# Expert layers in tiles of 128 slots, with each expert's split weights kept in a ring and rows scattered into slot order

## The reference, cut

```python
# L0: 16 experts, 4 choices, inner size 256, and one shared expert
scores = sigmoid(xf @ gate_w.T); s = scores + gate_bias
...
comb = zeros((T, E)).at[arange(T)[:, None], idx].add(weights)
h = silu(einsum('td,eid->tei', xf, w1)) * einsum('td,eid->tei', xf, w3)
y = einsum('tei,edi,te->td', h, w2, comb)
z = silu(xf @ ws1.T) * (xf @ ws3.T) @ ws2.T        # the shared expert
# L1: 8 experts, 2 choices, inner size 1024
topk_scores, topk_idx = top_k(einsum('btd,ed->bte', x, gate_w), 2)
hidden = silu(h1) * h2                # h1, h2: halves of x @ w12[e].T
y = sum(softmax-weighted hidden @ w3[e].T)
x = x + y + z                         # xf, x above: layer norm of x
```

## Time and profile before

| | us |
|---|---|
| median of 3 runs | 2283.02 |
| lowest, highest | 2277.21, 2283.86 |
| the profiled execution, own time | 2267.15 |
| its span in the trace | 2264.7 |

### The profile page before, as it was taken

One profiled execution on the slowest core, in us unless ns is written; L12 is line 12 of the kernel. 1 busy time (PEld: TensorE's weight loads), 2 busy tenths in 40 slices (PEclk: granted clock), 3 DMA queues, 4 the chain that ended last, 5 costly groups with the idle time before them and its releaser, 6 DMA issues. The chain is left out here.

```text
span 2264.7 us, 44300 instructions
## 1 busy us (share of the span) xinstructions
PE 1938.3 (86%) x16818; PEld 1669.7 (74%) x16818; DVE 1024.7 (45%) x1792; ACT 950.6 (42%) x1594; POOL 911.7 (40%) x655
## 2 busy tenths in 40 slices
PE   6876898738999991999999999777849999999993
PEld 5445676537999991788888888555639999999993
DVE  5445443465555566133333333355534445454442
ACT  2112333415666662233333333343425555555551
POOL 0004321006777774433333333221016666566653
PEclk9897999868999996999999999867869999999997
DMA  6562010007888885211011010100035566565653
GB/s 246 215 242 79 20 57 1 21 21 281 277 281 276 281 264 201 67 39 39 28 37 37 28 37 19 43 6 24 1 115 208 203 215 214 201 218 203 214 187 120
DMA packets 102161, 298.19 MB, mean 132 GB/s; under 512 B 10896, under 2 KB 27920, under 8 KB 102064
## 3 DMA queue, kind: packets, MB, share of 16 engines
q1 hardware_dynamic: 76192, 231.57, 29.4%
q0 software_dynamic: 11840, 38.81, 5.7%
q10 hardware_dynamic: 14032, 26.48, 3.1%
HBM read 264.32 MB, written 32.51 MB: 131 GB/s over the span
## 5 line engine op out<-in xcount | busy, mean ns | idle before, releaser
L133 PE MATMUL banks<-ra 128*128 128x256 f32 (+2 forms) x2940 | 963.1, 328 | 39.0 <-DVE ra L1133 10.4
L134 PE MATMUL banks<-ra 128*128 128x256 f32 (+2 forms) x2940 | 946.2, 322 | 0.0
L135 PE MATMUL banks<-ra 128*128 128x256 f32 (+2 forms) x2940 | 943.0, 321 | 0.0
L133 PEld LDWEIGHTS banks<-ra 128*128 128x128 f32 x2940 | 568.1, 193 | 95.5 <-DVE ra L1133 16.3
L135 PEld LDWEIGHTS banks<-ra 128*128 128x128 f32 x2940 | 568.2, 193 | 41.4
L134 PEld LDWEIGHTS banks<-ra 128*128 128x128 f32 x2940 | 569.5, 194 | 33.9
L1588 POOL TENSOR_TENSOR ra<-fa,ra 128x1024 fp32r<-128x1024 f32 x187 | 446.1, 2386 | 237.7 <-ACT ra L1621 236.6
L1621 ACT ACTIVATE ra<-fa 128x1536 fp32r<-128x1536 f32 x190 | 281.5, 1482 | 84.9 <-DMA fa<-in_L_units 67.5
L1705 DVE TENSOR_TENSOR ra<-fa,ra 128x256 fp32r<-128x256 f32 x190 | 162.1, 853 | 91.9 <-ACT ra L1645 91.9
L1680 DVE TENSOR_TENSOR ra<-fa,ra 128x512 fp32r<-128x512 f32 x190 | 133.7, 703 | 115.3 <-ACT ra L1621 108.8
L308 POOL TENSOR_TENSOR ra<-fa,ra 128x2048 fp32r<-128x2048 f32 (+2 forms) x19 | 71.8, 3788 | 258.0 <-ACT ra L302 228.8
(11 more groups left out here) (277 smaller groups left out, 2259.9 us busy)
## 6 DMA issues: line engine op xcount, KB each, us to landing
fa<-in_L_units SPq DMA_DIRECT2D x190, 768.0 KB, 4.2
fa<-in_ctxT SPq DMA_DIRECT2D x48, 514.0 KB, 4.1
ea_y_scratch<-fa ACTq DMA_DIRECT2D x35, 512.0 KB
fa_cross<-in_ctxT SPq DMA_DIRECT2D x16, 514.0 KB, 8.3
fa<-in_ctx SPq DMA_DIRECT2D x16, 512.0 KB, 6.6
fa_cross<-in_ctx SPq DMA_DIRECT2D x16, 512.0 KB, 7.0
eb_y_scratch<-fa ACTq DMA_DIRECT2D x15, 512.0 KB, 3.4
fa<-in_L_attn_w_qkvT SPq DMA_DIRECT2D x6, 1024.0 KB, 6.7
```

The source lines that it names most:

```text
L133: pe.matmul(psum, lh, rh, start=first, stop=False)
L134: pe.matmul(psum, lh, rl, start=False, stop=False)
L135: return pe.matmul(psum, ll, rh, start=False, stop=last)
```

## The change

Lines named "after" are those of the changed kernel; there mm3 is L128 to L130, the weights' high part on ScalarE L1570, the rows' load L1574 and high part L1579, the SiLU L1609, `turn` L1729 and the scatter L1535.

- **Tiles of 128 slots.** 47 routed and 8 shared tiles in L0 (four shared ones first, four last) and 23 in L1; 110 and 184 pairs of tile and unit.
- **Roles in the matmul.** The rows and the hidden layer are stationary, the weights moving. `up` is 12 matmuls of 256 columns, both halves side by side. The hidden layer now comes out with tokens on partitions, so TensorE transposes it (`turn_h`, L1781 after), and VectorE makes its high part (a copy from PSUM) and its low part. `down` is 3 matmuls of 512 columns.
- **Weights once per expert.** SyncE loads each nonempty expert's units once, 36 in L0 and 64 in L1, through three or two staging buffers. The split units live in a ring of 8 or 12 slots. The first ring's units are split by ScalarE and VectorE, every later one by GpSimd alone (L1556 and L1558 after, 1536 columns each), after a wait on the expert's last tile, whose number it reads into a register.
- **Addresses by register.** For each routed tile TensorE's queue reads a count and one (L0) or two (L1) offsets from SBUF, and addresses the weights through registers. VectorE makes these tables with some 26 small operations at the start of `experts`. In L1 the first weights are loaded after them, and ScalarE splits all 12 first units ahead of its wait for the rows.
- **Rows in slot order.** The normed rows stay in SBUF. Once the slots are known, GpSimd scatters them to DRAM (`sorted`, 32 scatters in L0, 16 in L1), and ScalarE's queue loads each tile's rows with a plain DMA. `sorted` is first filled with zeros (12.3 MB in L0, 6.0 MB in L1) by one DMA; the routing block ends only after it. ScalarE waits for all scatters ahead of its tile loop. `normed_scratch` and the one-hot products are gone.
- **End of L0.** All 32 gathers follow the last store of a routed tile; the shared expert's result is added to x straight from PSUM.
- The loops over pairs of tiles are written out; the SBUF areas are allocated anew for each part of the program (hence the suffixes `_C` for L0's and `_F` for L1's expert layer; `rest_` holds float32 data, `rest_r_` the split rows and hidden layer, `weights_` the ring).

The core of the diff:

```diff
-                    for n in range(W - 1):
-                        weights_low(n, n)
...
+                    for t in range(NT):
+                        for k in range(K):
+                            pool.indirect_dma_start(plan.sorted, bass.IndirectOffsetOnAxis(
+                                ap=plan.slot.bitcast(U32)[:, k, t:t + 1], axis=0), plan.xn[t], None).then_inc(plan.s_scattered, 16)
+                    eng.wait_ge(s_tables, 1)
+                    eng.wait_ge(s_split, R)
...
+                    for n in range(R, units):
+                        e, q = divmod(n - R, U)
+                        hi, lo = ring(n)
+                        eng.wait_ge(plan.s_ld[n % STAGED], 16 * (n // STAGED + 1))
...
+                            if q == 0 or at is None:
+                                at = eng.value_load(plan.end.bitcast(U32)[0:1, e - plan.first:e - plan.first + 1], min_val=0,
+                                                    max_val=U * TILES)
+                            eng.wait_ge(s_y, at + (q + 1))
...
+                        pool.tensor_copy(hi, plan.staging[n % STAGED]).then_inc(s_pair, 1)
+                        eng.wait_ge(s_pair, n - R + 1)
+                        pool.tensor_tensor(lo, plan.staging[n % STAGED], hi.bitcast(F32), ALU.subtract).then_inc(s_split, 1)
```

```diff
+                eng.wait_ge(s_zeros, 1)
+                eng.dma_start(plan.sorted.rearrange("(j p) d -> p j d", p=P),
+                              zeros.unsqueeze(1).to_broadcast([P, J, D])).then_inc(plan.s_zeroed, 16)
...
+                    start = 2 if plan.shared else R
+                    for n in range(start):
+                        weights_high(n)
+
+                    eng.wait_ge(s_tables, 1)
+                    eng.wait_ge(plan.s_scattered, 16 * K * NT)
+                    load_rows(0)
+                    load_rows(1)
+                    if not plan.shared:
+                        rows_high(0)
...
+                            eng.wait_ge(s_ht, n + 1)
+                            if n >= 2:
+                                eng.wait_ge(s_y, U + n - 1)
+                            dve.tensor_copy(hh_[b], banks[:, TB + b, 0:P]).then_inc(s_hh, 1)
+                            eng.wait_ge(s_hh, n + 1)
+                            dve.tensor_tensor(hl[b], banks[:, TB + b, 0:P], hh_[b].bitcast(F32),
+                                              ALU.subtract).then_inc(s_hl, 1)
```

More of the change, by code:

```diff
@@ L1237, in __init__ @@
                 self.layer, self.experts, self.choices = layer, (E0, E1)[layer], (K0, K1)[layer]
-                self.routed = (self.choices * T + self.experts * (CAP - 1)) // CAP
-                self.shared = layer == 0
-                self.kinds = self.choices + self.shared
-                self.tiles = self.routed + (T // CAP if self.shared else 0)
-                self.units = (I0, I1)[layer] // P
-                f = Area(fa, F_SIZE)
-                self.slot = f.take(self.kinds, NT)
-                self.weight = f.take(self.kinds, NT)
@@ L1247, in __init__ @@
-                self.token = f.take(2 * self.tiles)
-                self.expert = f.take(self.tiles)
-                self.at = f.at
-        def routing(tag, plan, norm):
-            layer, E, K = plan.layer, plan.experts, plan.choices
-            KN, H = plan.kinds * NT, 2 * plan.tiles
-            f = Area(fa, F_SIZE, plan.at)
+                self.routed = (self.choices * T + self.experts * (P - 1)) // P
+                self.shared = NT if layer == 0 else 0
+                self.units = U = (I0, I1)[layer] // P
@@ new lines, in __init__ @@
+                self.slots = (8, 12)[layer]
+                self.groups, self.group = ((4, 2), (3, 4))[layer]
+                assert self.groups * self.group == self.slots
+                self.first = 1 if self.shared else 0
+                self.ranks = self.experts + 2 * self.first
+                self.offsets = U // self.group
+                self.staged = S_ = (3, 2)[layer]
+                f = self.area = Area(rest, REST)
+                self.xn = [f.take(D) for _ in range(NT)]
+                self.staging = [f.take(3 * D) for _ in range(S_)]
@@ new lines, in __init__ @@
+                self.slot = f.take(self.choices, NT)
+                self.weight = f.take(self.choices, NT)
+                self.count = f.take(self.routed)
+                self.offset = f.take(self.offsets, self.routed)
+                E = self.experts
+                self.end, self.expert = f.take(E), f.take(E)
+                self.tiles, self.before, self.tri, self.ids = f.take(E), f.take(E), f.take(E, E), f.take(E)
+                self.numbers, self.rank_offset = f.take(self.routed), f.take(self.offsets, E + 3)
@@ new lines, in __init__, with load_unit @@
+                self.small = f.take(64)
+                self.s_ld = [sem(f"e{layer}_loaded{b}") for b in range(S_)]
+                self.s_zeroed, self.s_scattered = gather_sem(f"e{layer}_zeroed"), gather_sem(f"e{layer}_scattered")
+                self.sorted = nc.dram_tensor(f"e{layer}_sorted", [self.routed * P, D], F32, kind="Internal").ap()
+            def load_unit(self, eng, w, n, expert):
+                b = n % self.staged
+                eng.dma_start(self.staging[b], w[expert * self.units + n % self.units]).then_inc(self.s_ld[b], 16)
@@ L1255, in routing @@
+        def routing(tag, plan, norm, w):
+            layer, E, K, J = plan.layer, plan.experts, plan.choices, plan.routed
+            f, r = Area(temps, TEMPS), Area(temps_r, TEMPS_R)
+            gate_high, gate_low, kept = r.take(DC, P), r.take(DC, P), r.take(NT, E)
+            zeros = f.take(D)
             gate, gbias = f.take(DC, P), f.take(E)
@@ L1777, in cross_heads @@
+                            down(i, q, wt)
+                        wt = ahead
         def cross_heads():
```

682 lines of the change are left out of this document (353 added, 329 removed).

## The result

The changed kernel takes 2450.7 us (median of 4 runs, 2448.3 to 2452.8) against 2280.1 us before (4 runs): a ratio of 1.075, 95% interval 1.072 to 1.078. Slower was forecast, but by 68 us, not by 171, and the time lies above the range.

What follows compares the result with a forecast made beforehand. The prediction took TensorE's matmuls to bound both expert layers. It summed +44 us in L0 and +24 us in L1 to +68 us, giving 2351 us on the median of 2283.02, range 2250 to 2425.

Steps and rivals of the forecast that it cites:

- the chain of transpose, copy and subtraction: In each unit, between the hidden tile's transpose and "down": 0.98 us, against a cover of 6 matmuls, 0.71 us.
- The unit of 2.57 us: Period of one unit in the expert tiles: 2.49 us plus 0.08 us for register steps.
- The 0.08 us for the register steps: TensorE's queue, 10 register steps per unit in routed tiles: bounds 0 and 0.46 us, 0.08 us taken.
- the 4.4 of the text for a less pressed GpSimd: GpSimd's split of each later weight unit: about 6.0 us with gaps, 4.4 us if less pressed.
- one such read is 0.276 us and the register operation behind it 0.152, about 0.45 us together: TensorE's reads between routed tiles: three in L1, 1.34 us, counted as +0.85 us; two in L0, +0.4 us.
- the shared tiles, 20 us, hide half: End of L0: the last four shared tiles, 20 us, hide half of the 40 us of 32 gathers.
- The fill with zeros: L0's routing end waits for 12.3 MB: 49 us at 281 GB/s, taken; 47 us later at 144 GB/s.
- The start of L1: Tables, then six pairs of weight units at 7.6 us, then rows: first product 35.6 us later, at 1735.8.
- The dense stream: Rival: the waits per unit vanish and loads and register steps run ahead, 2.24 us a unit; 2188 us, chance 0.15.
- The registers cost nothing: Rival: the chain stays but register steps are free, L1 tile 20.9 us, L0 5.9; 2291 us, chance 0.18.
- The rival of a GpSimd that sets the pace: GpSimd needs 8 us a unit, +60: 2411 us; chance 0.13 together with a slow fill or TensorE's queue at its upper bound.
- the reads' upper bound: L1's reads between tiles with nothing hidden: the full 1.34 + 0.3 us per tile.

Runs made afterwards that it cites:

- constant-address tiles: Changed kernel with the real routing's addresses as program constants, so TensorE's queue reads no counts or offsets and sets no address registers: 2286.2 us.
- the early order: Changed kernel with the same reads moved ahead to where TensorE waits for VectorE anyway: 2307.6 us.

## Why the forecast was wrong, point by point

- **Direction and mechanism.** Slower, for three stated reasons, each seen: the chain of transpose, copy and subtraction, the reads between tiles, and the starts and the end of L0 that nothing hides. The unit of 2.57 us came out at 2.58, "down" starts 0.24 us later than in a dense stream where 0.2 was worked out, and the constant-address tiles take 20.8 and 5.8 us where the working gives 20.9 and 5.9. The 0.08 us for the register steps was a choice between 0 and 0.46 us; that it came out is in part luck. GpSimd took 1.47 + 3.48 us a unit, less than the 6.0 worked out (the 4.4 of the text for a less pressed GpSimd has no row), and held TensorE up in three places only, for 4.7 us in all.
- **The step that failed: "one such read is 0.276 us and the register operation behind it 0.152, about 0.45 us together".** That was SyncE's row. On TensorE's queue a read lasts 0.30 us (L1) or 0.55 (L0's first), and from one to the next it is 0.65 us in L1 and 0.90 in L0. The forecast also hid 0.8 us under the running "down" and gave 0.3 back: +0.85 us for an L1 tile. Measured is 1.9 us: the next product comes 2.57 us after "down" began, and its three matmuls take 0.69 us of that. The Trainium skill (DMA: Bandwidth & Descriptors, section Latency and other measured facts) gives a floor of about 600 ns for tensor_load; the prediction set it aside for the trace's 276 ns. A single read's duration is below it here as well, but the 0.65 us from read to read in L1 lie close to it, and that is what a tile pays.
- **What had no term: the clock behind the gap.** I priced a gap as idle time alone. Among the gaps of 1.6 to 1.75 us in L1 and 1.0 to 2.0 in L0 the granted clock fell in about every other tile of L1 and every third of L0, and the products until it rose again started 0.21 us apart instead of 0.12. In L1 this is the alternation of 23.3 and 24.4 us. It is the smaller part, some 31 us of the two layers. With gap and clock, a read-free or read-early tile is 2.4 to 3.1 us shorter in L1 and 1.9 to 2.1 in L0: 164 us by constants, 143 by the early order. Together these two points are the +68 and +34 us of the table.
- **The last shared tiles: "the shared tiles, 20 us, hide half" of the gathers.** They took 58 us. The forecast put what the gathers do to the tiles beside them at nothing, without a reason, and the runs show that these gathers delay TensorE's signals; moving them behind the tiles gives 17 us, and 38 is what the tiles lost. The gathers' own 40 us came out as worked out (931.3 to 971.1). The sums did not: the forecast left four additions and the statistics behind the gathers, 7.7 us, and in the trace all 32 additions and the statistics stand behind the last shared tile, 27 us.
- **The fill with zeros** went at 324 GB/s, above both rates that the prediction priced (281 and 144). It landed at 480.9, before the routing's last operation on VectorE (483.1), and did not delay it; the start of L0 was 8 us earlier than forecast.
- **The start of L1** was right in mechanism and within 5 us (95.3 against 90.4): a split unit took 3.9 us, 3.8 was worked out.
- **The rivals.** The dense stream (2188 us) did not come: every unit waits for the subtraction, and only twelve matmuls of cover instead of six bring the period to 2.24 us, which is the dense value of the working. Its terms, 514 - 424 and 353 - 268, add up to 175 us, not to the 171 of the text; and 110 units of 2.13 us are 234 us, not 230. Neither enters the forecast. "The registers cost nothing" (2291 us) falls by the 0.08 us a unit that constant addresses take away; its time is close to that run's only because its tile of 20.9 us leaves out the reads as well, as that run does.
- **The range** reached to 2425 us. It took the reads' upper bound as 1.34 + 0.3 us, worked out from the same wrong row, and no bound at all for gathers beside tiles. The rival of a GpSimd that sets the pace stood for "slower still"; the real cause of slower still was neither that nor the fill.

## What to carry to other kernels

Reads from SBUF into registers that stand in a row cost what it takes from read to read on that engine's queue (here 0.65 to 0.90 us on TensorE, where SyncE's row of durations had suggested 0.45), and here they cost nothing where the engine waited for another anyway: spread such reads over units with a wait instead of putting them where the next work is ready. When operands change roles so that a result needs a transpose and two copies before its next use, count the matmuls between the transpose and that use; here 6 gave 2.58 us a unit and 12 gave 2.24. Price every gap of TensorE with the clock that may follow it (here 1.1 to 1.2 us for a tile in which it fell). And a wait that is taken away may uncover the next one on the same queue, as at the start of L0: look up what stands behind it.

## What the runs showed of the hardware, beyond what was expected

- Gaps of 1.6 to 1.75 us on TensorE once per tile of some 24 us (L1), or of 1.0 to 2.0 us once per tile of 8 us (L0), went with a stretch at the lower level of the clock in 12 of 23 and 15 of 46 tiles (mean clock 0.96 and 0.93); with gaps of 0.5 us or less inside the tiles it stayed at 1.00.
- On TensorE's queue, register steps between a subtraction's end and the matmul that waits for it made the handoff 0.14 us instead of 0.05; the other steps of a unit were hidden beside running matmuls.
- Beside GpSimd's indirect DMAs, 1.25 us apart, TensorE's signals to VectorE and ScalarE came up to 23 us late in this program, whether the DMAs wrote inside or outside the memory that TensorE reads; beside plain DMAs of the same 8 MB they did not. VectorE's signal to TensorE was not late. In the kernel before, the same kind of gathers did no harm. The cause is open.
- A fill of 12.3 MB in one DMA out of a broadcast tile ran at 324 GB/s.
